# The ternary feed-forward phase of a two-layer transformer kernel: every second batch is rounded and clamped by POOL ahead of the turn

## The chip, the cores and the metric

The kernel runs on one core of one Trainium2 chip. The metric is device time in microseconds of one execution, as a median of several runs. Four engines compute: PE (TensorE, matrix products and transposes), ACT (ScalarE), DVE (VectorE) and POOL (GpSimd). They run their own instruction streams and meet at semaphores. SBUF is the on-chip memory that all of them reach; PE writes its results to PSUM.

## The reference, cut to what matters

Sixteen batches of 128 tokens with 128 features go through two layers, each a cross attention and a feed-forward part. The change touches only the last one, the feed-forward part of the second layer, whose activations are quantised to whole numbers:

```python
def _act_quant(x):
    scale = 127.0 / jnp.clip(jnp.max(jnp.abs(x), axis=-1, keepdims=True), 1e-05)
    xq = jnp.clip(jnp.round(x * scale), -128.0, 127.0) / scale
    return x + jax.lax.stop_gradient(xq - x)
...
gate = jax.nn.silu(_bitlinear(x, w_gate))        # 128 -> 512
up = _bitlinear(x, w_up)                         # 128 -> 512
return _bitlinear(gate * up, w_down)             # 512 -> 128, of the quantised product
```

So of every batch the product gate * up, 128 tokens by 512, gets one maximum per token, is multiplied by 127 over that maximum, rounded, clamped to -128..127, and multiplied with the last weight.

## The kernel before, in words

`main_kernel` calls five phases one after the other: `context`, `attention` of layer 0, `experts`, `attention` of layer 1, and `ternary_ffn`. The last is the one that the change edits. It begins at about 383 us of the span and holds all that follows.

`ternary_ffn` is a software pipeline over the 16 batches. Each engine has a function `step(h, r)`, and `run` (L1557) calls it for h = 0 to 20: steps 0 to 3 lie between the `head` parts, which turn and copy the input of four batches at a time, steps 4 to 7 are written out, steps 8 to 15 are two rounds of a hardware loop of four steps (`Fori`), and steps 16 to 20 are written out again. In step h each engine works on other batches, always in this order:

- PE: `gate_and_up` of batch h (L1711, L1712: two products 128x128 by 128x512 into `ps_gf` and `ps_uf`), `down` of batch h-5 (L1725: four products of the quantised, turned batch with the last weight, into `ps_df`), `turn` of batch h-3 (L1718: four transposes of `gr` into `ps_tf`).
- ACT: `copy_gu` of batch h-4 (L1679: `ps_tf` to `gq_t` in SBUF as bf16, with MAGIC subtracted), `round_gu` of batch h-3 (L1672: `gu` times `g_inv` plus MAGIC into `gr`; adding 1.5 times 2 to the 23rd leaves a float with no fraction, which is the rounding), `silu` of batch h (L1665: `ps_gf` to `gate`).
- DVE: `product` of batch h-1 (L1606: `ps_uf` times `gate` into `gu`), `clamp_gu` of batch h-4 (L1625: `gq_t` in place, bf16), `maximum` of batch h-1 (L1611), `tail` of batch h-5 (L1630: `ps_df` times `g_out`, added to `x_all`), and in each even step `scales` for two batches at once (L1618 `g_scl`, L1621 `g_inv`).
- POOL: once for two batches `g_out`, from `g_scl` (L1580), 128x2. Nothing else in the steps.
- SP stores a batch when its tail is done (L1743).

The buffers tie the engines: `gr`, `gq_t`, `gate` and each PSUM tile have two slots, `gu` has four. The clamp runs behind the turn, on the copied bf16 tile; since the transposed numbers are the rounded ones, it can stand on either side of it. An even batch is one with an even number; its scales come with those of the odd batch behind it.

Of the kernel before, what the change touches and what calls it, by code (L numbers as in the profile page):

```python
# [14 lines left out]
B = 16  # L15
# [1510 lines left out]
def ternary_ffn(nc, t, c):  # L1526
# [4 lines left out]
    with ExitStack() as ph:  # L1531
# [3 lines left out]
        def sem(name):  # L1535
# [15 lines left out]
            sem("clamp_ready"), sem("xt_done_f"), sem("xt_ready_f"))  # L1551
        gu_done, gate_ready, gu_ready, gmax_ready, gscl_step, gr_ready, gc_ready = (
            sem("gu_done"), sem("gate_ready"), sem("gu_ready"), sem("gmax_ready"), sem("gscl_step"), sem("gr_ready"), sem("gc_ready"))
        gt_done, gt_ready, d_done, out_ready = sem("gt_done"), sem("gt_ready"), sem("d_done"), sem("out_ready")
# [17 lines left out]
        @block.gpsimd  # L1572
        def _(pool):
            inputs.root(pool, NG - 1)
            w_down = c["w_scale"][:, 2:3].to_broadcast([P, 2])
            with pool.Fori(0, B // 4) as i:
                for pair in range(2):

                    pool.wait_ge(gscl_step, i * 4 + 2 * pair + 1)
                    pool.tensor_tensor(g_out[:, 2 * pair:2 * pair + 2], g_scl[:, 2 * pair:2 * pair + 2], w_down, ALU.mult)\  # L1580
                        .then_inc(out_scaled, 2)

        @block.vector
        def _(dve):
# [17 lines left out]
            def product(b, r):  # L1602
                wait(dve, gate_ready, b + 1)

                wait(dve, gr_ready, b - 3)
                dve.scalar_tensor_tensor(out=gu[:, r, :], in0=ps_u[:, r % 2, :], scalar=inputs.up_scl[:, bass.ds(b, 1)],  # L1606
                                         in1=gate[:, r % 2, :], op0=ALU.mult, op1=ALU.mult).then_inc(gu_ready, 1)

            def maximum(b, r):
                wait(dve, gu_ready, b + 1)  # L1610
                dve.tensor_reduce(g_max[:, r:r + 1], gu[:, r, :], AX_X, ALU.max, apply_absolute_value=True)\  # L1611
                   .then_inc(gmax_ready, 1)

# [12 lines left out]

# [21 lines left out]
        def _(act):  # L1648
# [43 lines left out]
        def _(pe):  # L1692
# [96 lines left out]
```

## Time and profile before

| What | us |
|---|---|
| median of 3 runs (lowest, highest) | 433.83 (432.37, 436.69) |
| the profiled execution: its time | 434.39 |
| its span, first to last instruction | 432.7 |
| of it the last phase, from about 383.2 on | 49.5 |
| product of the first and of the last batch start at | 388.29 and 421.02 |
| last instruction of DVE ends at | 430.45 |

The trace is of the profiled execution, and the times of its rows are microseconds from the start of the span. The execution's time is 1.7 us more than its span, and 0.56 us above the median. A view of busy time adds up instructions that can overlap at their ends: an instruction often starts before the one ahead of it on its engine has ended, so distances from start to start tell what an instruction takes out of its engine's time, and durations tell when a waiting engine may go.

### The profile page before, as it was taken

The numbers are of one execution on the slowest core, as the hardware profiler recorded it, in microseconds if no ns is written. First come the engines' busy times: TensorE is split into PE (matmuls) and PEld (weight loads), VectorE is DVE, ScalarE is ACT, GpSimd is POOL, SyncE is SP. The second block draws the span as 40 slices with busy tenths as digits, with TensorE's granted clock in tenths as the row PEclk, the third lists the DMA queues.
The fourth block names the chain that finished last, engine by engine and source line by source line (L and its number), as shares of the span: only waits on it lengthen the run. The fifth ranks groups of instructions, "written<-read, shape, count | busy, mean of one in ns | idle before, by whom it ended". The sixth has DMA issues, their size and how long they took to land. (4 is left out here: it accounts for less than half of the span.)

```text
span 432.7 us, 10420 instructions
## 1 busy us (share of the span) xinstructions
PE 359.2 (83%) x3434; PEld 258.3 (60%) x3434; DVE 288.3 (67%) x905; ACT 224.6 (52%) x420; POOL 90.2 (21%) x163
## 2 busy tenths in 40 slices
PE   2684779887877999999999999799899999756654
PEld 0452667776753677677767777566677676534433
DVE  6765768998946553663442443687789799367993
ACT  2152436665654745434343344055556656648993
POOL 7335131020211102101001001133333343310000
PEclk9886769999996999999999999889999999857996
DMA  7664954433144001630170100113443331000111
GB/s 215 138 157 111 226 165 129 130 117 111 55 124 148 2 2 40 126 80 2 36 208 12 36 0 0 37 31 104 122 127 113 101 100 28 3 1 1 32 30 37
DMA packets 54100, 34.98 MB, mean 81 GB/s; under 512 B 38744, under 2 KB 46256, under 8 KB 54064
## 3 DMA queue, kind: packets, MB, share of 16 engines
q1 hardware_dynamic: 44032, 31.43, 26.8%
q10 hardware_dynamic: 10032, 3.08, 3.0%
q8 instruction: 20, 0.33, 0.3%
q14 instruction: 16, 0.13, 0.1%
HBM read 24.60 MB, written 9.44 MB: 79 GB/s over the span
## 5 line engine op out<-in xcount | busy, mean ns | idle before, releaser
L1040 ACT ACTIVATE probs<-ps_e 128x512 f32<-128x512 f32 x128 | 74.6, 594 | 54.2 <-PE ps_e L885 49.7
L958 DVE TENSOR_REDUCE neg<-ps_s 128x4 f32<-128x512 f32 x128 | 85.1, 684 | 21.6 <-PE ps_s L868 20.1
L1286 DVE SCALAR_TENSOR_TENSOR x_all<-ps_ym,c_g,x_all 128x128 f32 (+1 forms) x128 | 36.0, 344 | 63.2 <-PE ps_ym L1381 63.0
L1381 PEld LDWEIGHTS ps_ym<-w,hid 128*128 128x128 f32 x512 | 60.8, 192 | 9.2 <-issue 6.7
L868 PE MATMUL ps_s<-k_rows,q_rows 96*128 96x128 bf16 x512 | 54.2, 234 | 10.6 <-DVE neg L958 4.9
L1381 PE MATMUL ps_ym<-w,hid 128*128 128x128 f32 x512 | 62.2, 276 | 0.0
L1371 PE MATMUL ps_h<-tok_t,w 128*128 (+1 forms) x128 | 62.1, 608 | 0.0
L1488 ACT ACTIVATE hid<-ps_h,b 128x512 f32<-128x512 f32 x64 | 43.1, 684 | 35.4 <-PE ps_h L1371 34.0
L868 PEld LDWEIGHTS ps_s<-k_rows,q_rows 96*128 96x128 bf16 x512 | 40.1, 104 | 24.1 <-issue 10.0
L885 PE MATMUL ps_e<-q_rows,k_rows 128*128 128x128 bf16 x512 | 51.2, 226 | 3.8 <-DMA q_rows<-neg_t 3.3
L885 PEld LDWEIGHTS ps_e<-q_rows,k_rows 128*128 128x128 bf16 x512 | 37.0, 101 | 9.1 <-DMA q_rows<-neg_t 3.9
L899 PE MATMUL ps_pv<-probs,v_aug 128*32 128x128 f32 x1024 | 36.5, 285 | 0.0
L1371 PEld LDWEIGHTS ps_h<-tok_t,w 128*128 128x128 f32 x128 | 22.6, 195 | 20.1 <-issue 14.9
L1093 POOL TENSOR_TENSOR v_aug<-v_all,zero 128x128 f32<-128x128 f32 x32 | 14.8, 463 | 88.4 <-PE ps_pv L899 87.2
L864 PE MATMUL ps_s<-upper,identb 128*128 128x512 bf16 x64 | 25.8, 403 | 4.6 <-PEq L1138 2.0
L899 PEld LDWEIGHTS ps_pv<-probs,v_aug 128*32 128x32 f32 x1024 | 27.0, 113 | 4.1 <-issue 0.4
L1052 ACT ACTIVATE neg_t<-ps_n 48x128 bf16<-48x128 bf16 x32 | 8.6, 269 | 35.3 <-PE ps_n L906 35.3
L1718 PE MATMUL ps_tf<-ident,gr 128*128 128x128 f32 x64 | 11.3, 303 | 14.2 <-ACT gr L1672 14.2
L925 PE MATMUL ps_y<-attn_w,oo_t 128*128 128x128 f32 x64 | 16.2, 336 | 7.5 <-ACT oo_t L1057 6.8
L984 DVE TENSOR_TENSOR x_all<-ps_y,x_all 128x128 f32<-128x128 f32 (+1 forms) x32 | 9.2, 287 | 16.7 <-PE ps_y L925 16.4
L1102 POOL TENSOR_SCALAR_AFFINE_SELECT probs<-probs 128x512 f32<-128x512 f32 x32 | 20.0, 625 | 0.0
L1045 ACT ACTIVATE o_t<-ps_pv 128x512 f32<-128x512 f32 x32 | 18.6, 580 | 2.1 <-PE ps_pv L899 2.0
(200 smaller groups left out, 555.7 us busy)
## 6 DMA issues: line engine op xcount, KB each, us to landing
k_rows<-k_dram SPq DMA_DIRECT2D x32, 144.0 KB
q_rows<-q_dram SPq DMA_DIRECT2D x32, 144.0 KB
k_rows<-k_dram SPq DMA_DIRECT2D x16, 288.0 KB
q_rows<-q_dram SPq DMA_DIRECT2D x16, 288.0 KB
k_dram<-parts SPq DMA_DIRECT2D x35, 128.0 KB, 2.5
w<-in_w SPq DMA_DIRECT2D x16, 128.0 KB, 2.7
q_dram<-parts SPq DMA_DIRECT2D x15, 128.0 KB, 2.2
q_dram<-parts ACTq DMA_DIRECT2D x9, 128.0 KB, 3.2
```

What stands on the lines that cost most here:

```text
L864: pe.matmul(ps_s[:, q % 2, :], identb[:], c["upper"][:].unsqueeze(1).to_broadcast([P, HQ, P]), start=True, stop=False, skip_group_check=True)
L868: last = pe.matmul(ps_s[:, q % 2, j * P:(j + 1) * P], q_rows[0:ROW_MAX, r, h, :], k_rows[0:ROW_MAX, r, h, :], start=(layer == 0), stop=Tru ...
L885: last = pe.matmul(ps_e[:, q % 2, j * P:(j + 1) * P], k_rows[:, r, h, :], q_rows[:, r, h, :], start=not masked, stop=True, skip_group_chec ...
L899: last = pe.matmul(ps_v[VW * j:VW * (j + 1), q * P:(q + 1) * P], v_aug[:, s, q * HQ + j, :], probs[:, s, q, j * P:(j + 1) * P], start=True ...
L958: dve.tensor_reduce(neg[:, s, q * HQ:(q + 1) * HQ], ps_s[:, q % 2, :].rearrange("p (h k) -> p h k", h=HQ), AX_X, ALU.max, negate=True).the ...
L1040: act.activation(probs[:, s, q, :], ps_e[:, q % 2, :], ACT.Exp, scale=SCALE).then_inc(exp_done, 1)
L1045: act.activation(o_t[:, s, :], ps_v[:], ACT.Copy).then_inc(ot_ready, 1)
L1102: pool.affine_select(out=probs[:, s, q, :], in_=probs[:, s, q, :], compare_op=ALU.is_ge, fill=0.0, base=0, pattern=[[0, HQ], [1, P]], chan ...
L1286: dve.scalar_tensor_tensor(out=batch_of(x_all, g * G + j), in0=ps_y[:, e % 2, j * D:(j + 1) * D], scalar=c_g[:, j, e:e + 1], in1=batch_of( ...
L1371: pe.matmul(ps_h[:, m, :], w1[:, e, m * P:(m + 1) * P], tok_t[:, bass.ds(g * GT, GT)], start=True, stop=True).then_inc(h_done, 1)
L1381: last = pe.matmul(ps_y[:, e % 2, j * D:(j + 1) * D], hid[:, (e % 2) * M + m, j * P:(j + 1) * P], w2[:, e, m, :], start=(m == 0), stop=(m ...
L1488: act.activation(hid[:, (e % 2) * M + m, :], ps_h[:, m, :], ACT.Gelu, bias=b1[:, e * M + m:e * M + m + 1]).then_inc(h_ready, 1)
```

## The change

For odd batches the rounding moves from ACT to POOL, and the clamp moves from DVE, behind the turn, to POOL, ahead of it: POOL reads `gu`, writes slot 1 of `gr`, waits for that, and clamps slot 1 in place, between MAGIC-128 and MAGIC+127, in 32-bit floats. Even batches stay as they were. POOL's hardware loop becomes eight written-out rounds.

The semaphores follow. `even_ready` and `odd_ready` take the place of `gr_ready`; `scale_step` takes that of `gmax_ready` and `gscl_step`, and `g_out` now waits for both scale instructions where it waited for the first. The rounding of an even batch waits for the scales of its pair, as before. An odd `down` waits for ACT's copy and for the tail two batches earlier.

```diff
@@ POOL @@
-            with pool.Fori(0, B // 4) as i:
-                for pair in range(2):
-
-                    pool.wait_ge(gscl_step, i * 4 + 2 * pair + 1)
-                    pool.tensor_tensor(g_out[:, 2 * pair:2 * pair + 2], g_scl[:, 2 * pair:2 * pair + 2], w_down, ALU.mult)\
-                        .then_inc(out_scaled, 2)
+            for pair in range(B // 2):
+                b, r = 2 * pair + 1, 2 * (pair % 2) + 1
+
+                pool.wait_ge(scale_step, 2 * b + 2)
+                pool.tensor_tensor(g_out[:, r - 1:r + 1], g_scl[:, r - 1:r + 1], w_down, ALU.mult).then_inc(out_scaled, 2)
+
+                wait(pool, gt_done, b - 1)
+                pool.tensor_scalar(gr[:, 1, :], gu[:, r, :], g_inv[:, r:r + 1], MAGIC, ALU.mult, ALU.add).then_inc(odd_ready, 1)
+                pool.wait_ge(odd_ready, b)
+                pool.tensor_scalar(gr[:, 1, :], gr[:, 1, :], MAGIC + 127.0, MAGIC - 128.0, ALU.min, ALU.max).then_inc(odd_ready, 1)
@@ DVE @@
-                wait(dve, gr_ready, b - 3)
+                if r % 2 == 0:
+                    wait(dve, even_ready, b - 2)
+                else:
+                    wait(dve, odd_ready, b - 3)
...
-                if exists(h - 4):
+                if exists(h - 4) and r % 2 == 0:
                     clamp_gu(h - 4, r % 2)
@@ ACT @@
-                if exists(h - 3):
+                if exists(h - 3) and (r - 3) % 2 == 0:
                     round_gu(h - 3, (r - 3) % 4)
@@ PE, turn @@
-                wait(pe, gr_ready, b + 1)
+                if s == 0:
+                    wait(pe, even_ready, b + 2)
+                else:
+                    wait(pe, odd_ready, b + 1)
@@ PE, down @@
-                wait(pe, gc_ready, b + 1)
+                if s == 0:
+                    wait(pe, gc_ready, b + 2)
+                else:
+                    wait(pe, gt_ready, b + 1)
+                    wait(pe, out_ready, b - 1)
```

What stands in a row on ACT in the middle of the hardware loop, two steps, before (`gq_t` is the copy, `gr` the rounding, `gate` the silu; the `L51` and `ISA` rows work out the value of a wait):

```order
L1679 ACTIVATE gq_t<-ps_tf,magic 128x512 [waits gt_done]
L1672 ACTIVATE gr<-gu,magic,g_inv 128x512 [waits gt_done,gscl_step]
L51 REGISTER_ALU
L1665 ISA [waits gu_ready,gu_done]
L1665 ACTIVATE gate<-ps_gf,in_gate_scl 128x512
L1679 ACTIVATE gq_t<-ps_tf,magic 128x512 [waits gt_done]
L1672 ACTIVATE gr<-gu,magic,g_inv 128x512 [waits gt_done,gscl_step]
L51 REGISTER_ALU
L1665 ISA [waits gu_ready,gu_done]
L1665 ACTIVATE gate<-ps_gf,in_gate_scl 128x512
```

And the same two steps now, an even step and an odd one:

```order
L1686 ACTIVATE gq_t<-ps_tf,magic 128x512 [waits gt_done]
L51 REGISTER_ALU
L1672 ISA [waits gu_ready,gu_done]
L1672 ACTIVATE gate<-ps_gf,in_gate_scl 128x512
L1686 ACTIVATE gq_t<-ps_tf,magic 128x512 [waits gt_done]
L51 ISA
L1679 ACTIVATE gr<-gu,magic,g_inv 128x512 [waits gt_done,scale_step_f]
L51 REGISTER_ALU
L1672 ISA [waits gu_ready,gu_done]
L1672 ACTIVATE gate<-ps_gf,in_gate_scl 128x512
```

The rounding is gone from the even step, in which batch h-3 is odd, and the copy and the silu follow each other there.

On DVE an even and an odd step in the middle of the loop stood like this before, from the product of one step to the tail of the next (`gu` is the product, `gq_t` the clamp, `g_max` the maximum, `x_all` the tail, `g_scl` and `g_inv` the scales):

```order
L1606 SCALAR_TENSOR_TENSOR gu<-ps_uf,in_up_scl,gate 128x512
L1625 TENSOR_SCALAR gq_t<-gq_t 128x512 [waits gt_ready]
L1611 TENSOR_REDUCE g_max<-gu 128x1 [waits gu_ready]
L1630 ISA [waits out_scaled,d_done]
L1630 SCALAR_TENSOR_TENSOR x_all<-ps_df,g_out,x_all 128x128
L1618 TENSOR_SCALAR g_scl<-g_max 128x2 [waits gmax_ready]
L1621 RECIPROCAL g_inv<-g_scl 128x2 [waits gscl_step]
L51 REGISTER_ALU
L1606 ISA [waits gr_ready,gate_ready]
L1606 SCALAR_TENSOR_TENSOR gu<-ps_uf,in_up_scl,gate 128x512
L1625 TENSOR_SCALAR gq_t<-gq_t 128x512 [waits gt_ready]
L1611 TENSOR_REDUCE g_max<-gu 128x1 [waits gu_ready]
```

And now:

```order
L1613 SCALAR_TENSOR_TENSOR gu<-ps_uf,in_up_scl,gate 128x512
L1632 TENSOR_SCALAR gq_t<-gq_t 128x512 [waits gt_ready]
L1618 TENSOR_REDUCE g_max<-gu 128x1 [waits gu_ready]
L1637 ISA [waits out_scaled,d_done]
L1637 SCALAR_TENSOR_TENSOR x_all<-ps_df,g_out,x_all 128x128
L51 REGISTER_ALU
L1625 TENSOR_SCALAR g_scl<-g_max 128x2 [waits scale_step_f]
L51 REGISTER_ALU
L1628 RECIPROCAL g_inv<-g_scl 128x2 [waits scale_step_f]
L1613 SCALAR_TENSOR_TENSOR gu<-ps_uf,in_up_scl,gate 128x512
L1618 TENSOR_REDUCE g_max<-gu 128x1 [waits gu_ready]
```

The clamp is gone from the odd step, the even step keeps it, and two register instructions have come in ahead of the scales.

On POOL, which had one instruction a pair, three now stand for every pair of batches:

```order
L1580 TENSOR_TENSOR g_out<-g_scl,w_scale 128x2 [waits scale_step_f]
L1583 TENSOR_SCALAR gr<-gu,g_inv 128x512 [waits gt_done]
L1585 TENSOR_SCALAR gr<-gr 128x512 [waits odd_ready]
L1580 TENSOR_TENSOR g_out<-g_scl,w_scale 128x2 [waits scale_step_f]
L1583 TENSOR_SCALAR gr<-gu,g_inv 128x512 [waits gt_done]
L1585 TENSOR_SCALAR gr<-gr 128x512 [waits odd_ready]
```

The two `TENSOR_SCALAR` rows are what left ACT and DVE; they lie between the `g_out` of one pair and that of the next.

## Rows read from the trace of the kernel before

**Rows 1.** Waits between 400 and 420 us: who waited, total us, times, longest.

```profile
PE ps_tf L1718 <- ACT gr L1672: 7.3, 9, 0.8
```

**Rows 2.** Timeline, ACT and PE in one step of the loop: start, duration, then idle before.

```profile
404.08 0.69 ACT L1679 ACTIVATE gq_t<-ps_tf,magic 128x512 bf16<-128x512 f32 x1 [0.17 <-PE ps_tf L1718]
404.67 0.80 ACT L1672 ACTIVATE gr<-gu,magic,g_inv 128x512 f32<-128x512 f32 x1
405.37 0.67 ACT L1665 ACTIVATE gate<-ps_gf,in_gate_scl 128x512 f32<-128x512 f32 x1
405.52 0.66 PE L1718 MATMUL ps_tf<-ident,gr 128*128 128x128 f32 x4 [0.82 <-ACT gr L1672]
406.22 0.69 ACT L1679 ACTIVATE gq_t<-ps_tf,magic 128x512 bf16<-128x512 f32 x1 [0.17 <-PE ps_tf L1718]
```

**Rows 3.** Timeline, DVE in two steps of the loop, even and odd; POOL beside it.

```profile
404.16 0.75 DVE L1606 SCALAR_TENSOR_TENSOR gu<-ps_uf,in_up_scl,gate 128x512 f32<-128x512 f32 x1 [0.35 <-ACT gate L1665]
404.83 0.28 DVE L1625 TENSOR_SCALAR gq_t<-gq_t 128x512 bf16<-128x512 bf16 x1
405.03 0.68 DVE L1611 TENSOR_REDUCE g_max<-gu 128x1 f32<-128x512 f32 x1
405.62 0.34 DVE L1630 SCALAR_TENSOR_TENSOR x_all<-ps_df,g_out,x_all 128x128 f32 x1
405.88 0.15 DVE L1618 TENSOR_SCALAR g_scl<-g_max 128x2 f32<-128x2 f32 x1
406.07 0.17 DVE L1621 RECIPROCAL g_inv<-g_scl 128x2 f32<-128x2 f32 x1
406.35 0.75 DVE L1606 SCALAR_TENSOR_TENSOR gu<-ps_uf,in_up_scl,gate 128x512 f32<-128x512 f32 x1
...
407.82 0.34 DVE L1630 SCALAR_TENSOR_TENSOR x_all<-ps_df,g_out,x_all 128x128 f32 x1
408.33 0.75 DVE L1606 SCALAR_TENSOR_TENSOR gu<-ps_uf,in_up_scl,gate 128x512 f32<-128x512 f32 x1 [0.17 <-ACT gate L1665]
...
406.18 0.19 POOL L1580 TENSOR_TENSOR g_out<-g_scl,w_scale 128x2 f32<-128x2 f32 x1 [4.01 <-DVE g_scl L1618]
```

**Rows 4.** Timeline, DVE in the written-out steps ahead of the loop.

```profile
395.41 0.75 DVE L1606 SCALAR_TENSOR_TENSOR gu<-ps_uf,in_up_scl,gate 128x512 f32<-128x512 f32 x1 [1.06 <-ACT gate L1665]
...
401.79 0.17 DVE L1621 RECIPROCAL g_inv<-g_scl 128x2 f32<-128x2 f32 x1
401.87 0.75 DVE L1606 SCALAR_TENSOR_TENSOR gu<-ps_uf,in_up_scl,gate 128x512 f32<-128x512 f32 x1
```

**Rows 5.** Groups of POOL's instructions, whole span: count | busy us, mean ns.

```profile
L1102 POOL TENSOR_SCALAR_AFFINE_SELECT probs<-probs 128x512 f32<-128x512 f32 x32 | 20.0, 625 | 0.0
L225 POOL TENSOR_TENSOR q_rest<-q_full,parts 128x512 f32<-128x512 f32 x4 | 4.6, 1160 | 46.6 <-ACT q_full L220 46.6
L195 POOL TENSOR_TENSOR q_rstd<-q_vareps,half 128x4 f32<-128x4 f32 x4 | 4.0, 1009 | 46.8 <-DVE q_vareps L101 46.8
L1580 POOL TENSOR_TENSOR g_out<-g_scl,w_scale 128x2 f32<-128x2 f32 x8 | 1.6, 194 | 36.6 <-DVE g_inv L1621 19.4 <-DVE g_scl L1618 17.1
```

**Rows 6.** Timeline near 54 us, POOL and DVE side by side.

```profile
52.41 4.51 POOL L1115 TENSOR_TENSOR x_all<-x_all,row_bias 128x2048 f32<-128x2048 f32 x1
...
53.80 0.69 DVE L958 TENSOR_REDUCE neg<-ps_s 128x4 f32<-128x512 f32 x1 [0.21 <-PE ps_s L868]
...
54.53 2.42 DVE L965 CAST neg_parts<-neg 128x16 bf16<-128x16 f32 x1
```

**Rows 7.** Timeline of DVE and PE behind the last product.

```profile
421.02 0.75 DVE L1606 SCALAR_TENSOR_TENSOR gu<-ps_uf,in_up_scl,gate 128x512 f32<-128x512 f32 x1
...
423.13 0.17 DVE L1621 RECIPROCAL g_inv<-g_scl 128x2 f32<-128x2 f32 x1
...
427.23 1.11 PE L1718 MATMUL ps_tf<-ident,gr 128*128 128x128 f32 x4 [1.05 <-ACT gr L1672]
...
430.10 0.35 DVE L1630 SCALAR_TENSOR_TENSOR x_all<-ps_df,g_out,x_all 128x128 f32<-128x128 f32 x1 [0.44 <-PE ps_df L1725]
```

More of the change, by code:

```diff
@@ L1551, in ternary_ffn @@
             sem("clamp_ready"), sem("xt_done_f"), sem("xt_ready_f"))
-        gu_done, gate_ready, gu_ready, gmax_ready, gscl_step, gr_ready, gc_ready = (
-            sem("gu_done"), sem("gate_ready"), sem("gu_ready"), sem("gmax_ready"), sem("gscl_step"), sem("gr_ready"), sem("gc_ready"))
+        gu_done, gate_ready, gu_ready, scale_step, even_ready, odd_ready, gc_ready = (
+            sem("gu_done"), sem("gate_ready"), sem("gu_ready"), sem("scale_step_f"), sem("even_ready"), sem("odd_ready"), sem("gc_ready"))
         gt_done, gt_ready, d_done, out_ready = sem("gt_done"), sem("gt_ready"), sem("d_done"), sem("out_ready")
@@ L1611, in maximum @@
                 dve.tensor_reduce(g_max[:, r:r + 1], gu[:, r, :], AX_X, ALU.max, apply_absolute_value=True)\
-                   .then_inc(gmax_ready, 1)
+                   .then_inc(scale_step, 1)
             def scales(b, r):
                 pair = slice(r - 1, r + 1)
-                wait(dve, gmax_ready, b + 1)
+                wait(dve, scale_step, b * 2)
                 dve.tensor_scalar(g_scl[:, pair], g_max[:, pair], 1e-5, 1.0 / 127.0, ALU.max, ALU.mult)\
-                   .then_inc(gscl_step, 1)
-                wait(dve, gscl_step, b - 1 + 1)
-                dve.reciprocal(g_inv[:, pair], g_scl[:, pair]).then_inc(gscl_step, 1)
+                   .then_inc(scale_step, 1)
+                wait(dve, scale_step, b * 2 + 1)
+                dve.reciprocal(g_inv[:, pair], g_scl[:, pair]).then_inc(scale_step, 1)
             def clamp_gu(b, s):
                 wait(dve, gt_ready, b + 1)
-                dve.tensor_scalar(gq_t[:, s, :], gq_t[:, s, :], 127.0, -128.0, ALU.min, ALU.max).then_inc(gc_ready, 1)
+                dve.tensor_scalar(gq_t[:, s, :], gq_t[:, s, :], 127.0, -128.0, ALU.min, ALU.max).then_inc(gc_ready, 2)
             def tail(b, r):
@@ L1668, in round_gu @@
             def round_gu(b, r):
-                wait(act, gscl_step, b + 2 - r % 2)
+                wait(act, scale_step, b * 2 + 4)
                 wait(act, gt_done, b - 1)
                 act.activation(gr[:, r % 2, :], gu[:, r, :], ACT.Identity, bias=magic[:, 0:1], scale=g_inv[:, r:r + 1])\
-                   .then_inc(gr_ready, 1)
+                   .then_inc(even_ready, 2)
             def copy_gu(b, s):
```

## The prediction, made blind

> **What bounds the phase now.** I read the waits between engines first, then the timeline of one step, engine by engine, since the change lies wholly in the last 49.5 us. In the waits PE stands 7.3 us of 20 for ACT's rounding [rows 1]. The timeline shows the ring behind it: copy at 404.08, rounding at 404.67, turn at 405.52, next copy at 406.22 [rows 2]. One step is 406.22 - 404.08 = 2.14 us: 0.59 from copy to rounding, 0.80 + 0.05 until the turn starts, 0.66 for the turn, 0.04 until the copy may start. ACT stands idle 0.17 of it. So ring and ACT are nearly equal: ACT alone needs 0.59 + 0.70 + (0.85 - 0.17 = 0.68) = 1.97.
>
> DVE is almost as full. Its even step, with the scales, is 406.35 - 404.16 = 2.19 us and waits for nothing; its odd step is 408.33 - 406.35 = 1.98, with a wait for ACT's silu in it [rows 3]. So the reader is to see two full engines and a ring, 4.27 us for two steps, and a DVE that sets the limit as soon as ring and ACT are relieved.
>
> **ACT and PE after the change.** A rounding (0.70 from start to start) leaves every second step. ACT then needs 2 x 0.59 + 2 x 0.68 + 0.70 = 3.24 us for two steps. The ring through ACT and PE is broken at odd batches. PE issues the same work; its odd `down` waits for the tail two batches earlier, which DVE does two steps before, so I cost this wait at nothing; behind it in PE's queue is the turn of an odd batch, and if the wait did bind, the copy would be late by as much.
>
> **DVE after the change.** Even step: unchanged at 2.19. Two register instructions come ahead of the scales and one may come ahead of the product. They are hidden where the engine is still busy with the tail; otherwise each can cost about 0.06 (the loop costs 0.20 for its register work: reciprocal to product is 406.35 - 406.07 = 0.28 in the loop [rows 3], but 401.87 - 401.79 = 0.08 outside of it [rows 4]). I take 0.06 for the pair, between 0 and 0.12. Odd step: the clamp goes, but what it frees is small. Product to maximum is 405.03 - 404.16 = 0.87 with the clamp between; without it the maximum still waits for the product's end, 0.75 + 0.04 = 0.79. So a clamp of 0.28 busy gives back 0.08. The step is 0.79 + 0.59 (maximum to tail) + tail to next product. That last term is hidden behind a wait in the trace: at least 0.26 (tail to `g_scl`), at most 0.51 (407.82 to 408.33) [rows 3]. I take 0.26 + 0.20 of register work = 0.46, so 1.84. Two steps: 2.19 + 1.84 + 0.06 = 4.09.
>
> - Loop, product 7 to product 15: 421.02 - 404.16 = 16.86 now [rows 3, 7], 4 x 4.09 = 16.36 then: -0.5 (bounds -1.5 with 0.26 and no register cost, 0 if DVE stays as long as the ring).
> - Written-out steps, product 3 to product 7: 404.16 - 395.41 = 8.75 now [rows 3, 4]. Without register work a pair is (2.19 - 0.20) + (0.79 + 0.59 + 0.26) = 3.63, two are 7.26. The first clamp still waits for the same copy and product 7 may wait for its silu, so I count -1.3 of the -1.5.
>
> **The tail.** Now: last product 421.02, end of the last tail 430.10 + 0.35 = 430.45, so 9.43 [rows 7]. In it ACT rounds batches 13, 14 and 15 one behind the other, each in the ring. Then: the reciprocal ends 423.13 + 0.17 - 421.02 = 2.28 behind the product. ACT rounds batch 14 at once (2.32 to 3.12), PE turns it from 3.17, at up to the 1.11 of the last turn (0.66 in the loop: PE's matrix clock has fallen there), so until about 4.2 [rows 2, 7]. Meanwhile POOL starts `g_out` 0.15 behind its releaser (406.18 against 405.88 + 0.15) and needs 0.19 [rows 3], and then twice d, the unknown duration of its new instructions, with 0.05 behind each: batch 15 is ready at 2.28 + 0.15 + 0.19 + 0.10 + 2d = 2.72 + 2d. With d = 0.75 that is 4.2, equal to PE. From turn to end the rows give 430.45 - 427.23 = 3.22 [rows 7], less a clamp and its wait, 0.28 + 0.04 [rows 3]: 2.90. Total 7.1 to 7.2: -2.25.
>
> **POOL's instructions.** The trace has none of this kind. Nearest from below is a one-input instruction of the same 128x512 floats, in place, at 0.625 us; from above a two-input one at 1.160 us [rows 5]. Rounding has one tensor input and a scalar per token, clamping one tensor input and two constants, so I go near the lower row: d = 0.85. That it may lie outside is shown by the power on 128x4, 1.009 us for four columns [rows 5]: this engine's price hangs on the operation. Against d = 0.75 my value costs 2 x 0.1 in the tail: +0.2.
>
> POOL's work must also fit. Counted from the reciprocal's start: 0.17 + 0.15 + 0.15 (`g_out`, its overlap off) + d + 0.05 + d = 0.52 + 2d. The next even step's clamp on DVE comes 0.28 + 1.84 + 0.67 = 2.79 after it, and the turn, which waits for POOL, about there too. So up to d = 1.13 nothing is late but the tail. This clamp is what counts, for the trace shows that POOL can hold DVE up: a CAST of 128x16 took 2.42 us, from 54.53 to 56.95, while a POOL instruction ran from 52.41 to 56.92; a reduction beside the same instruction took its usual 0.69 [rows 6]. Products, maxima and tails read at most one tensor from SBUF, like that reduction from PSUM; clamp and `g_scl` are of the CAST's kind.
>
> The Trainium skill says so as a rule ("SBUF — State Buffer", Who interferes with whom): a DVE instruction in a two-port mode and a GpSimd instruction exclude each other for their whole length, and reductions never contend. Rows 6 agree (2.42 us against 0.69). It leaves the sum at d = 0.85, where POOL is done 0.57 before the clamp, but it sets where rival 2 begins: with it at d = 1.13; without it only POOL's own ring of two instructions, a turn of 0.66 and three waits of 0.05 would have to stay under 4.09, so up to d = 1.64.
>
> **Sum.** -1.3 - 0.5 - 2.25 + 0.2 = -3.85 us. The profiled execution is 434.39, so 430.5; it lies 0.56 above the median, and from the median 433.83 the same step leads to 430.0. I give 430.2.
>
> **Rivals** (from 433.8).
> 1. DVE gains nothing in the loop: tail to product is 0.51 or more and the registers show, so a pair stays near 4.27. For it: DVE waits only 0.17 in an odd step [rows 3]. Against it: even then the written-out steps and the tail gain. Time: with half of the written-out steps' gain, 0.65, and 2.05 in the tail it is 431.1; with 1.3 in all, 432.5. Chance 0.2.
> 2. POOL is the new bound, the case on the other side. From d = 1.13 on each pair is longer by 2d - 2.27, since DVE's clamp has to wait for POOL, and with it all of DVE's queue. Over some 6.5 pairs and with 2(d - 0.75) in the tail: d = 1.16 gives +0.3 + 0.8 on top of -4.05, so 430.9; d = 1.37 gives +3.1 + 1.2, no gain left, 434; d = 1.6 gives +6.0 + 1.7, so 437.5. Above 1.37 the kernel is slower than before. For it: the 1.160 and 1.009 rows; against it: 0.625. Chance that d exceeds 1.37: 0.15, that it exceeds 1.65 (over 1% slower): 0.1. A rule of the Trainium skill leads here ("GPSIMD Engine Reference", Key points): for elementwise work DVE is about twice as fast. DVE reads a 128x512 float tile in 0.68 in its reduction [rows 3]; twice that would be an estimate of 1.36 for d, just the point where nothing is gained. The same page's section Engine selection calls one-input work roughly line-rate, and the 0.625 row agrees with that.
> 3. More than forecast: no register cost, tail to product 0.3, PE still at its full clock in the tail. -1.5 - 1.3 - 2.6 = -5.4: 428.4. Chance 0.1.
>
> The forecast (429 to 431.2) has 0.55. One per cent, about what a measurement here can tell from no change, is 4.3 us, and my sum ends short of it: of the forecast's chance I count 0.2 beyond the line, and rival 3's 0.1. So faster 0.3, within 1% 0.6, slower 0.1. The range 428.8 to 434.8 leaves out some 0.08 below and 0.12 above.
>
> **What would show it.** Right: roundings on ACT eight, PE's wait for them about halved, DVE waiting for almost nothing in the loop with a pair near 4.1; POOL's two instructions at 0.65 to 1.1 each; the last turn within 5 us of the last product, the last clamp gone from the chain. Wrong: `TENSOR_SCALAR` on POOL above 1.2, DVE clamps of over 0.5 that end with a POOL instruction, or the turn of odd batches waiting for POOL; and for rival 1 a DVE pair at 4.25 with no waits.

## The result, and the profile after

The changed kernel ran in 428.60 us in the median of four runs (426.15 to 431.78), the kernel before in 434.38 (432.37 to 436.69) beside it. The ratio is 0.9854, with an interval of 0.981 to 0.9897: faster, by 4.5 to 8.2 us, where I had 3.85. A second, longer comparison, told of below, gave 0.988 (0.9838 to 0.9922). Ratios, here and below, leave out runs that lay over 1.5% above the fastest of their kernel. The profiled execution took 427.59 us with a span of 425.9, against 434.39 and 432.7.

So 6.8 us of span are gone. I cut both traces at the same instructions to see where:

| Stretch, us | before | after | change | predicted |
|---|---|---|---|---|
| start of the last phase (first instruction of DVE in it) | 383.26 | 380.77 | -2.49 | 0 |
| from there to the first product | 5.03 | 5.04 | 0 | 0 |
| product 0 to product 3 | 7.12 | 6.68 | -0.44 | 0 |
| product 3 to product 7, written-out steps | 8.75 | 8.77 | 0 | -1.3 |
| product 7 to product 15, hardware loop | 16.86 | 15.62 | -1.24 | -0.5 |
| last product to the end of the last tail | 9.43 | 6.55 | -2.88 | -2.05 |

Two things catch the eye. A third of the gain lies ahead of the phase, in code that the change leaves alone. And inside the phase no term that I had priced has the size that I gave it: their sum, -4.5, is near my -3.85 only because the misses have both signs.

The waits that bound the kernel before, in the view that answers to [rows 1], here for 400 to 416 us:

```profile
PE ps_tf L1728 <- ACT gr L1679: 5.7, 4, 1.4
ACT gr L1679 <- DVE g_inv L1628: 0.9, 2, 0.5
```

PE waits for ACT's rounding four times in these 16 us, where it was seven times before, but each wait is longer, and the total is 5.7 us both times: the sum of PE's waits does not show the gain, and the sign "PE's wait for them about halved" came in their number alone. What is new is the second row: ACT now waits for DVE's reciprocal, which it never did before in this phase.

DVE in two steps of the loop, to be laid beside [rows 3]:

```profile
404.93 0.34 DVE L1637 SCALAR_TENSOR_TENSOR x_all<-ps_df,g_out,x_all 128x128 f32 x1
405.19 0.74 DVE L1613 SCALAR_TENSOR_TENSOR gu<-ps_uf,in_up_scl,gate 128x512 f32<-128x512 f32 x1
405.91 0.29 DVE L1632 TENSOR_SCALAR gq_t<-gq_t 128x512 bf16<-128x512 bf16 x1
406.12 0.68 DVE L1618 TENSOR_REDUCE g_max<-gu 128x1 f32<-128x512 f32 x1
406.72 0.34 DVE L1637 SCALAR_TENSOR_TENSOR x_all<-ps_df,g_out,x_all 128x128 f32 x1
406.97 0.16 DVE L1625 TENSOR_SCALAR g_scl<-g_max 128x2 f32<-128x2 f32 x1
407.17 0.17 DVE L1628 RECIPROCAL g_inv<-g_scl 128x2 f32<-128x2 f32 x1
407.45 0.75 DVE L1613 SCALAR_TENSOR_TENSOR gu<-ps_uf,in_up_scl,gate 128x512 f32<-128x512 f32 x1
408.23 0.69 DVE L1618 TENSOR_REDUCE g_max<-gu 128x1 f32<-128x512 f32 x1
408.84 0.34 DVE L1637 SCALAR_TENSOR_TENSOR x_all<-ps_df,g_out,x_all 128x128 f32 x1
409.10 0.74 DVE L1613 SCALAR_TENSOR_TENSOR gu<-ps_uf,in_up_scl,gate 128x512 f32<-128x512 f32 x1
409.77 0.29 DVE L1632 TENSOR_SCALAR gq_t<-gq_t 128x512 bf16<-128x512 bf16 x1
```

No row names a wait. The even step, 405.19 to 407.45, is 2.26 (2.19 before), the odd one, 407.45 to 409.10, is 1.65 (1.98 before). Two steps are 3.91, where I had 4.09. Read the odd step by its parts: product to maximum 0.78 (I had 0.79), maximum to tail 0.61 (0.59), tail to next product 0.26, where I had taken 0.46. That one number is nearly the loop's whole miss; with the 0.01 of the maximum and 2.26 for my 2.25 it gives 0.18 a pair.

ACT and PE beside it; shown are the rounding of an even batch, its turn and its copy:

```profile
407.42 0.81 ACT L1679 ACTIVATE gr<-gu,magic,g_inv 128x512 f32<-128x512 f32 x1 [0.46 <-DVE g_inv L1628]
408.29 0.66 PE L1728 MATMUL ps_tf<-ident,gr 128*128 128x128 f32 x4 [1.38 <-ACT gr L1679]
408.98 0.69 ACT L1686 ACTIVATE gq_t<-ps_tf,magic 128x512 bf16<-128x512 f32 x1 [0.17 <-PE ps_tf L1728]
```

The rounding starts 0.08 behind the end of DVE's reciprocal (407.17 + 0.17), and the copy ends at 409.67, 0.10 ahead of the clamp at 409.77 that needs it. So the ring of waits did not vanish: it now runs from DVE's reciprocal through ACT and PE to DVE's next clamp. The experiments come back to it.

POOL's groups, from 380 us on, for [rows 5]:

```profile
L1583 POOL TENSOR_SCALAR gr<-gu,g_inv 128x512 f32<-128x512 f32 x8 | 5.5, 691 | 0.0
L1585 POOL TENSOR_SCALAR gr<-gr 128x512 f32<-128x512 f32 x8 | 4.9, 613 | 0.7
```

The unknown of the prediction is known: 0.691 us for the rounding, 0.613 for the clamp. The clamp takes about what the affine select on a tile of that size took, 0.625. The kernel before also has this same instruction, two constants on 128x512 floats, on DVE, where it takes 0.415; POOL needs 1.5 times that:

```profile
L1590 DVE TENSOR_SCALAR tok_tk<-tok_tk 128x512 f32<-128x512 f32 x4 | 1.7, 415 | 0.0
```

The end, for [rows 7]:

```profile
416.88 0.74 DVE L1613 SCALAR_TENSOR_TENSOR gu<-ps_uf,in_up_scl,gate 128x512 f32<-128x512 f32 x1
...
418.81 0.17 DVE L1628 RECIPROCAL g_inv<-g_scl 128x2 f32<-128x2 f32 x1
...
419.93 0.66 PE L1728 MATMUL ps_tf<-ident,gr 128*128 128x128 f32 x4 [1.62 <-ACT gr L1679]
...
420.74 0.91 PE L1728 MATMUL ps_tf<-ident,gr 128*128 128x128 f32 x4
...
423.08 0.35 DVE L1637 SCALAR_TENSOR_TENSOR x_all<-ps_df,g_out,x_all 128x128 f32<-128x128 f32 x1 [0.32 <-PE ps_df L1739]
```

The two last turns follow each other at once, at 0.66 and 0.91 us, where the last one before took 1.11 and stood alone. The second of them starts at 420.74, 0.06 behind POOL's last clamp (420.07 to 420.68): it is POOL's chain, and not the turn of batch 14, that ends last in the tail.

### The profile page after: what moved, and what is told of

It reads as the page before. It is cut to its first block and busy times, and to the rows that moved or that the text cites. A ratio compares the mean times of both kernels' runs of the same rounds, so it can differ in the third digit from the quotient of the medians.

```text
span 425.9 us, 10418 instructions
## 1 busy us (share of the span) xinstructions
PE 354.5 (83%) x3432; PEld 255.7 (60%) x3434; DVE 286.5 (67%) x897; ACT 219.1 (51%) x412; POOL 100.6 (24%) x179
## 5 line engine op out<-in xcount | busy, mean ns | idle before, releaser
L1093 POOL TENSOR_TENSOR v_aug<-v_all,zero 128x128 f32<-128x128 f32 x32 | 14.7, 462 | 88.1 <-PE ps_pv L899 87.0
L912 PE MATMUL ps_o<-ident,o_t 128*128 128x128 f32 x128 | 19.7, 277 | 0.0
```

The costliest lines, as they stand in the source:

```text
L912: last = pe.transpose(ps_o[:, q * P:(q + 1) * P], o_t[:, s, q * P:(q + 1) * P], ident[:])
```

## The experiments

Each trace is measured between the same instructions as the first two. "Clock" is PE's mean granted clock between product 3 and 7, and behind the last product; 1.00 is the 2.4 GHz level, 0.50 the level of 1.2 GHz.

| Kernel | ratio to before (interval) | phase starts | 3 to 7 (clock) | 7 to 15 | tail (clock) | whole phase |
|---|---|---|---|---|---|---|
| before | | 383.26 | 8.75 (1.00) | 16.86 | 9.43 (0.70) | 47.19 |
| before, again | 0.9976 (0.9937, 1.0014) | 380.45 | 9.59 (0.82) | 16.87 | 9.06 (0.82) | 47.21 |
| changed | 0.9854 (0.981, 0.9897) | 380.77 | 8.77 (0.74) | 15.62 | 6.55 (0.82) | 42.66 |
| changed, again | 0.988 (0.9838, 0.9922) | 380.79 | 7.80 (1.00) | 15.61 | 6.09 (1.00) | 41.65 |
| round only | 0.9895 (0.9857, 0.9934) | 382.25 | 8.07 (1.00) | 15.97 | 6.24 (1.00) | 42.42 |
| clamp only | 1.0187 (1.0139, 1.0236) | 382.43 | 11.55 (0.58) | 21.07 | 10.60 (0.66) | 55.36 |
| one clamp more | 0.9865 (0.9821, 0.991) | 381.52 | 7.81 (0.82) | 15.92 | 7.00 (0.87) | 42.41 |
| two clamps more | 0.9938 (0.9901, 0.9976) | 383.44 | 8.79 (0.74) | 16.62 | 8.15 (0.69) | 45.28 |
| no clamp | 0.983 (0.9791, 0.9868) | 379.74 | 8.03 (0.74) | 15.08 | 5.83 (1.00) | 40.86 |
| 15 alone on POOL | 0.9962 (0.9932, 0.9992) | 381.13 | 9.51 (0.82) | 16.89 | 7.88 (0.64) | 46.43 |
| 13 and 15 on POOL | 0.9919 (0.9888, 0.9951) | 383.17 | 9.24 (0.82) | 16.86 | 7.25 (0.77) | 45.50 |
| written out, before | 0.9995 (0.996, 1.003) | 381.42 | 10.37 (0.50) | 17.53 | 9.53 (0.69) | 49.36 |
| written out, changed | 0.9886 (0.9843, 0.9928) | 383.99 | 7.64 (1.00) | 15.43 | 6.29 (1.00) | 41.51 |
| written out, no clamp | 0.981 (0.9758, 0.9862) | 384.05 | 7.00 (1.00) | 14.24 | 6.14 (0.83) | 39.53 |

### Does the change act ahead of its phase? Both kernels again

No edit in either.

> The kernel before, unchanged, once more. In the first pair of traces 6.8 us of span went, of which only 4.5 lie in the last phase (383.26 to 430.45 before, 380.77 to 423.43 after); the other 2.3 lie ahead of it, where both kernels are the same. Theory A (that part is chance, set by where PE's clock falls near the end of the second attention): ratio 1.00 within 0.5%, and the start of the last phase moves by 1 us or more against 383.26 in this trace, while the distance of product 7 to product 15 stays 16.8 to 16.9 us and the tail 9.2 to 9.6. Theory B (the change also moves code or transfers ahead of the phase): the phase again starts at 383.0 to 383.5.

> The changed kernel, unchanged, with more rounds. Theory A: ratio 0.988 to 0.991, that is 4 to 5 us, what the phase alone gives, and the phase starts somewhere between 380.5 and 384. Theory B: ratio 0.984 to 0.986 and the phase starts at 380.5 to 381.2 again. By both product 7 to product 15 is 15.6 us (bound by DVE) and product 3 to product 7 is 8.8 if PE's granted clock is 0.5 in these steps as in the first trace of this kernel, but near 7.5 if it is 1.0.

Theory A holds by the kernel before: it now reaches the phase at 380.45, 2.8 us earlier than in its first trace, and with the same 47.2 us in the phase itself (its tail is 9.06, 0.1 under what I expected). Its medians in this comparison are 434.20 and 434.24. The changed kernel alone would not have decided: it started at 380.79, within 0.02 of its first trace, as theory B had it too. Over all fourteen traces of the table the start lies between 379.7 and 384.1 in no order that goes with the edits. The windows of 4 us near the end of the second attention show what part of it is. First trace of the kernel before (columns: length, then busy us and count of PE, PE's loads, DVE, ACT and POOL, then PE's clock and the transfers' share and rate):

```profile
368.00:372.00 4.00, 3.12 (x39) 2.55 (x42) 1.56 (x6) 2.69 (x7) 2.48 (x6) 0.78 0.01 3
372.00:376.00 4.00, 3.48 (x41) 2.40 (x33) 0.78 (x4) 1.85 (x4) 1.46 (x4) 0.79 0.00 0
```

And its second trace:

```profile
368.00:372.00 4.00, 3.48 (x57) 2.75 (x57) 1.63 (x6) 2.85 (x8) 2.63 (x5) 1.00 0.01 3
372.00:376.00 4.00, 2.74 (x44) 1.95 (x44) 2.40 (x8) 3.01 (x7) 0.76 (x2) 1.00 0.02 4
```

The same code ran at a granted clock of 0.78 and 0.79 of full speed once, and of 1.00 the next time. What that costs is read between two additions that DVE makes in both traces, first trace, then second:

```profile
369.70 0.29 DVE L984 TENSOR_TENSOR x_all<-ps_y,x_all 128x128 f32<-128x128 f32 x1 [1.97 <-PE ps_y L925]
375.26 0.29 DVE L984 TENSOR_TENSOR x_all<-ps_y,x_all 128x128 f32<-128x128 f32 x1 [3.18 <-PE ps_y L925]
...
368.60 0.29 DVE L984 TENSOR_TENSOR x_all<-ps_y,x_all 128x128 f32<-128x128 f32 x1 [1.97 <-PE ps_y L925]
372.60 0.29 DVE L984 TENSOR_TENSOR x_all<-ps_y,x_all 128x128 f32<-128x128 f32 x1 [1.63 <-PE ps_y L925]
```

The stretch takes 5.56 us at a mean clock of 0.69, and 4.00 at 1.00. That is 1.6 of the 2.8 us; 1.1 were there at its start already. The changed kernel shows both too: 4.00 at 1.00 in its first trace, 5.55 at 0.69 in its second, which still starts the phase as early because it was 1.7 us ahead at the stretch's start.

So 2.5 of the 6.8 us between the first two traces say nothing on the change. Its own effect is the difference of the phase: 47.19 and 47.21 against 42.66 and 41.65, on the mean 5.0 us, or 1.2%. Both measured ratios have that in their intervals.

The second trace of the changed kernel settles the written-out steps too. Against the first trace of the kernel before, with the clock at 1.00 in both, product 3 to 7 is 8.75 before and 7.80 changed. The -1.3 that I gave this term was -0.95, and the zero of the first pair went with a low clock in the changed kernel:

```profile
394.00:398.00 4.00, 3.80 (x22) 2.63 (x21) 3.43 (x8) 3.26 (x6) 1.48 (x3) 0.61 0.02 5
```

in its first trace, against its second:

```profile
394.00:398.00 4.00, 2.46 (x21) 1.72 (x21) 3.76 (x10) 3.50 (x7) 1.48 (x3) 1.00 0.02 5
```

### Which half pays? Rounding alone, clamp alone

`round only`: POOL rounds the odd batches, and DVE clamps all of them as before (not shown: `down` again waits for the clamp of every batch).

```diff
-                pool.tensor_scalar(gr[:, 1, :], gu[:, r, :], g_inv[:, r:r + 1], MAGIC, ALU.mult, ALU.add).then_inc(odd_ready, 1)
-                pool.wait_ge(odd_ready, b)
-                pool.tensor_scalar(gr[:, 1, :], gr[:, 1, :], MAGIC + 127.0, MAGIC - 128.0, ALU.min, ALU.max).then_inc(odd_ready, 1)
+                pool.tensor_scalar(gr[:, 1, :], gu[:, r, :], g_inv[:, r:r + 1], MAGIC, ALU.mult, ALU.add).then_inc(odd_ready, 2)
...
-                if exists(h - 4) and r % 2 == 0:
+                if exists(h - 4):
                     clamp_gu(h - 4, r % 2)
```

> Changed kernel, but POOL only rounds the odd batches; DVE clamps all batches behind the turn as before. Theory A (DVE sets the pace once ring and ACT are relieved, and a clamp costs it only 0.09 to 0.2 a step): product 7 to product 15 is 15.9 to 16.7 us, between the two; tail 6.4 to 7.0, since POOL's clamp (0.66) and DVE's (0.34) there nearly exchange; ratio 0.989 to 0.992. Theory C (the clamp is what made the loop faster): product 7 to 15 is 16.8 or more.

Product 7 to 15 is 15.97, the tail 6.24, a little under what I expected. Theory A holds: relieving ACT brings 0.9 of the loop's 1.25, the clamp 0.35, which is 0.09 for each of four odd clamps, as product and maximum have it. In the whole phase, at full clock from product 3 on in both, the clamp is worth 42.42 - 41.65 = 0.8 us; the ratios, 0.9895 and 0.988, can't tell the two kernels apart. So most of the gain is the rounding's. The trace also shows the exclusion of [rows 6] at work. DVE's clamp of an odd batch and POOL's rounding beside it, DVE first:

```profile
397.12 0.58 DVE L1630 TENSOR_SCALAR gq_t<-gq_t 128x512 bf16<-128x512 bf16 x1
...
405.33 0.36 DVE L1630 TENSOR_SCALAR gq_t<-gq_t 128x512 bf16<-128x512 bf16 x1
```

and POOL:

```profile
396.86 0.69 POOL L1583 TENSOR_SCALAR gr<-gu,g_inv 128x512 f32<-128x512 f32 x1
...
404.84 0.70 POOL L1583 TENSOR_SCALAR gr<-gu,g_inv 128x512 f32<-128x512 f32 x1
```

The clamp takes 0.58 in place of 0.28 and ends at 397.70, 0.15 behind the end of POOL's rounding (397.55); the other one takes 0.36 and ends at 405.69, again 0.15 behind POOL's 405.54. All six clamps of this trace that start under a rounding of POOL do so: they take 0.36 to 0.58 and end 0.14 or 0.15 behind it. The changed kernel avoids it, since DVE has no clamp in the steps in which POOL works.

`clamp only`: ACT rounds all batches, and POOL clamps the odd ones in `gr`, ahead of the turn (not shown: which scales and which semaphore an odd rounding goes by).

```diff
-                wait(pool, gt_done, b - 1)
-                pool.tensor_scalar(gr[:, 1, :], gu[:, r, :], g_inv[:, r:r + 1], MAGIC, ALU.mult, ALU.add).then_inc(odd_ready, 1)
                 pool.wait_ge(odd_ready, b)
...
-                if exists(h - 3) and (r - 3) % 2 == 0:
+                if exists(h - 3):
                     round_gu(h - 3, (r - 3) % 4)
```

> Changed kernel, but ACT rounds all batches, as before; POOL only clamps the odd ones in gr ahead of the turn. If the ring of ACT and PE was the bound (rounding, turn, copy), POOL's clamp now stands inside it in every second step: about 0.61 + 0.15 longer for a pair, so product 7 to product 15 goes from 16.86 to 19 to 20 us and the ratio is 1.006 to 1.012. If DVE was the bound already (so that the clamp taken off it is what pays), product 7 to 15 falls to 16.4 or less and the ratio is below 0.998.

The sign is as the ring has it, the size is more than I expected: 21.07 for the loop, a ratio of 1.0187. The chain of waits shows POOL inside the ring, and a turn at the low clock level (1.13 for 0.66) behind 1.5 us in which PE had nothing to do; the granted clock between products 7 and 15 was 0.90 on the mean, against 1.00 in the loop of both main kernels:

```profile
412.13 0.81 ACT gr L1677
412.94 0.08 issue
413.02 0.62 POOL gr L1583
413.64 0.04 issue
413.69 1.13 PE ps_tf L1726 x4
```

So the clamp taken off DVE is worth nothing as long as ACT rounds all batches, and a POOL instruction in the path from rounding to turn costs more than its 0.61 us: the loop is 4.2 us longer than the kernel before's, 1.05 for each pair. How much of that is the low clock no run separates. The change works because POOL does the whole of an odd batch, beside ACT and not behind it.

### How much more could POOL take? The clamp issued again

```diff
                 pool.tensor_scalar(gr[:, 1, :], gr[:, 1, :], MAGIC + 127.0, MAGIC - 128.0, ALU.min, ALU.max).then_inc(odd_ready, 1)
+                pool.wait_ge(odd_ready, 4 * pair + 3)
+                pool.tensor_scalar(gr[:, 1, :], gr[:, 1, :], MAGIC + 127.0, MAGIC - 128.0, ALU.min, ALU.max).then_inc(odd_ready, 1)
```

with the counts that others wait for raised to four for each odd batch; the second form has this once more.

> Changed kernel with POOL's clamp issued twice (the second changes nothing), 0.66 us more on POOL for each pair. POOL is then done some 2.55 us behind the start of the reciprocal, just ahead of DVE's clamp of the next even step at 2.67. By my account of POOL's slack the loop keeps its time (product 7 to 15: 15.6 to 15.8) and only the tail grows by about 0.6: ratio 0.2% above that of the changed kernel. If POOL had no slack: product 7 to 15 grows by 0.5 or more for each pair, 17.5 or more.

> POOL's clamp issued three times, 1.35 us more a pair; POOL is busy until 3.25 us behind the reciprocal. Theory L (a POOL instruction keeps DVE's clamp waiting until it ends): DVE's clamps show durations or starts that end with POOL's third clamp, late by 0.5 to 0.7 in each pair; product 7 to product 15 is 17.5 to 18.8 us. Theory R (no such exclusion, only the ring POOL, turn, which is about 3.6 us for a pair and under 3.9): product 7 to 15 stays 15.6 to 16.0 and only the tail grows, by about 1.3.

One clamp more gives 15.92 in the loop, 0.1 above what I expected, and a tail of 7.00. The 0.3 lies in the loop's first pair, 4.37 us at a clock of 0.93; the other three, at 1.00, are 3.83, 3.89 and 3.83, no longer than the changed kernel's. The slack is there. Two more cost the loop 1.0 us, between the two theories' ranges, and neither theory has the reason. Theory L wanted DVE's clamps late behind POOL; their longest is 0.33. What happens is this. DVE first:

```profile
408.38 0.75 DVE L1617 SCALAR_TENSOR_TENSOR gu<-ps_uf,in_up_scl,gate 128x512 f32<-128x512 f32 x1 [0.44 <-ACT gate L1676]
412.96 0.29 DVE L1636 TENSOR_SCALAR gq_t<-gq_t 128x512 bf16<-128x512 bf16 x1
```

PE and ACT:

```profile
405.48 0.66 PE L1732 MATMUL ps_tf<-ident,gr 128*128 128x128 f32 x4 [0.99 <-POOL gr L1589]
406.18 0.69 ACT L1690 ACTIVATE gq_t<-ps_tf,magic 128x512 bf16<-128x512 f32 x1 [1.01 <-PE ps_tf L1732]
407.47 0.68 ACT L1676 ACTIVATE gate<-ps_gf,in_gate_scl 128x512 f32<-128x512 f32 x1
```

and POOL, the third clamp of the next pair:

```profile
413.01 0.71 POOL L1589 TENSOR_SCALAR gr<-gr 128x512 f32<-128x512 f32 x1
```

The odd turn at 405.48 waits for POOL, ACT's copy of it waits until 406.18, and the rounding and the silu, which have nothing to do with that batch, stand behind the copy in ACT's queue; so the product waits 0.44 for its silu. It is a wait passed on by an engine that works in order. The exclusion shows only the other way round: DVE's clamp began at 412.96, and POOL's, from 413.01, took 0.71 in place of 0.61. Rival 2's price was a pair longer by 2d - 2.27. With 0.69 + 3 x 0.61 = 2.52 for 2d that is 0.25 a pair, 1.0 for the loop's four, and 1.0 is what the loop lost; but it came by another path than the one I had named, every second pair being 4.4 us and the others 3.9, so the agreement is luck.

### The tail: batch 15 alone, then 13 and 15

The kernel before, with POOL doing batch 15, and in a second form also 13; the rest as before (`LAST` stands for these batches; in the second form POOL's hardware loop is written out as well):

```diff
+                        pool.wait_ge(gscl_step, b + 1)
+                        pool.wait_ge(gt_done, b - 1)
+                        pool.tensor_scalar(gr[:, 1, :], gu[:, b % 4, :], g_inv[:, b % 4:b % 4 + 1], MAGIC, ALU.mult, ALU.add)\
+                            .then_inc(xt_done, 1)
+                        pool.wait_ge(xt_done, done + 1)
+                        pool.tensor_scalar(gr[:, 1, :], gr[:, 1, :], MAGIC + 127.0, MAGIC - 128.0, ALU.min, ALU.max)\
+                            .then_inc(xt_done, 1)
...
-                if exists(h - 3):
+                if exists(h - 3) and not h - 3 in LAST:
                     round_gu(h - 3, (r - 3) % 4)
```

> Kernel before, with batch 15 alone rounded and clamped by POOL ahead of its turn; all others as before. If the tail's gain comes from batch 15 no longer standing behind batch 14 on ACT, and the loop's gain is another matter: last product to last tail falls from 9.43 to 6.5 to 7.0, product 7 to product 15 stays 16.8 to 16.9, the time falls by 2.5 to 3 us (ratio 0.993 to 0.995). If the tail is short in the changed kernel only since PE's clock holds longer there: the tail stays above 8 and the ratio is 0.997 or more.

> Kernel before, with batches 13 and 15 on POOL (15 alone brought the tail only from 9.06 to 9.43 down to 7.88, since batch 14's rounding still stood behind the turn and copy of 13 on ACT, and PE's granted clock had fallen by its turn). If that is the reason, with 13 off ACT too the rounding of 14 starts within 0.1 us of the reciprocal's end, its turn still runs at the high clock (0.66 us), and the tail is 6.1 to 6.8, as in the changed kernel; product 7 to 15 stays 16.7 to 16.9; the time falls by 2.4 to 3.0 us, ratio 0.993 to 0.995. If the short tail needs the rest of the change, it stays above 7.2.

Batch 15 alone gives 7.88, a gain of 1.2 to 1.6 us (from 9.06 or 9.43) where I expected 2.4 to 2.9, at a ratio of 0.9962. Batch 14's rounding still stood behind the turn and the copy of 13. With 13 on POOL too it starts at the reciprocal's end, but the tail is 7.25 and not 6.1 to 6.8, just above the 7.2 that I had set as the mark for "the short tail needs the rest of the change":

```profile
423.73 0.81 ACT L1682 ACTIVATE gr<-gu,magic,g_inv 128x512 f32<-128x512 f32 x1 [0.82 <-DVE g_inv L1631]
424.60 1.05 PE L1733 MATMUL ps_tf<-ident,gr 128*128 128x128 f32 x4 [1.58 <-ACT gr L1682]
```

The rounding is 0.03 behind the reciprocal (423.53 + 0.17), as it should be. The turn takes 1.05 instead of 0.66: in this run the clock had fallen by then, in the second trace of the changed kernel it stayed at 1.00 to the end. Against that trace, with its 6.09, the 1.16 us are mostly this: both last turns take 1.05 or 1.06 for 0.66 and the products behind them some 0.6 for 0.4. Another 0.2 is a reciprocal that ends 2.28 behind the last product in place of 2.11, behind a clamp of DVE that starts 0.85 behind the product in place of 0.68. So of the tail's 2.9 us some 1.8 to 2.2 are the order of work in the last batches (9.06 to 9.43 down to 7.25), and most of the rest goes with PE's clock. Whether the change holds the clock up is not shown. The eight traces in which POOL rounds every odd batch have 0.82 to 1.00 behind the last product, but for the 0.69 with two clamps more; the six in which ACT rounds in the loop have 0.64 to 0.82.

### Does DVE set the pace? Steps written out, clamps left out

```diff
-            with eng.Fori(2, B // 4) as i:
-                for j in range(4):
-                    step(i * 4 + j, j)
+            for h in range(8, B):
+                step(h, h % 4)
```

`no clamp` leaves out the clamp to -128..127, on POOL and on DVE. The largest value of a row is 127 by the division, so nothing is clipped. On POOL the rounding then counts for two, and every `down` waits as an odd one does (not shown).

```diff
-                pool.wait_ge(odd_ready, b)
-                pool.tensor_scalar(gr[:, 1, :], gr[:, 1, :], MAGIC + 127.0, MAGIC - 128.0, ALU.min, ALU.max).then_inc(odd_ready, 1)
...
-                if exists(h - 4) and r % 2 == 0:
-                    clamp_gu(h - 4, r % 2)
```

> Changed kernel without any clamp of the rounded products, on POOL or DVE (left out: the clamp to -128..127; the values are at most 127 already, since each row is divided by its own maximum, so the output does not change by it). If DVE sets the pace in the loop, an even step gets 0.09 shorter (product to maximum 0.78 in place of 0.86): product 7 to product 15 falls by 0.3 to 0.6 from 15.6, and the tail by 0.3 to 1.0 (POOL's 0.66 goes, PE's turn of batch 14 then comes last): ratio 0.2 to 0.3% below that of the changed kernel. If something else paces the loop, product 7 to 15 stays 15.6.

> Changed kernel with steps 8 to 15 written out, so that no register work stands ahead of the waits. Reciprocal to next product is 0.28 to 0.30 in the loop and 0.08 outside. If DVE paces the loop, each pair gets 0.2 shorter: product 7 to product 15 falls from 15.6 to 14.7 to 15.0 us, the time by 0.6 to 0.9 us. If ring or ACT pace it, it stays at 15.4 or more.

> Kernel before with steps 8 to 15 written out. If the ring ACT, PE paces it (2.135 us a step), product 7 to product 15 stays 16.7 to 17.0 and the ratio is 1.00 within 0.3%. If DVE's register work did, it falls by 0.6 or more.

> Changed kernel, written out and without the clamps (left out: the clamp to -128..127, which changes no value here). Product 7 to 15: 15.08 without clamps, less 0.8 by writing out: 14.2 to 14.5 us, if DVE still paces; tail 5.6 to 6.2. Time 425.5 to 426.5, ratio 0.978 to 0.982 to the kernel before. If ACT (3.24 us a pair and its waits) becomes the bound, product 7 to 15 stays at 14.8 or more.

The kernel before does not care: ratio 0.9995. Its loop read 17.53, missing its 16.7 to 17.0, because its first pair took 4.73 at a clock of 0.93; the last three pairs are 4.27, 4.27 and 4.26, the ring to the digit. The changed kernel cared less than expected: 15.43 in place of 14.7 to 15.0, and above the 15.4 that I had named as the sign of a ring. The written-out form shows why:

```profile
405.91 0.17 DVE L1627 RECIPROCAL g_inv<-g_scl 128x2 f32<-128x2 f32 x1
406.00 0.75 DVE L1612 SCALAR_TENSOR_TENSOR gu<-ps_uf,in_up_scl,gate 128x512 f32<-128x512 f32 x1
...
407.64 0.74 DVE L1612 SCALAR_TENSOR_TENSOR gu<-ps_uf,in_up_scl,gate 128x512 f32<-128x512 f32 x1
408.51 0.29 DVE L1631 TENSOR_SCALAR gq_t<-gq_t 128x512 bf16<-128x512 bf16 x1
...
409.77 0.17 DVE L1627 RECIPROCAL g_inv<-g_scl 128x2 f32<-128x2 f32 x1
```

and ACT's copy ahead of that clamp:

```profile
407.72 0.69 ACT L1685 ACTIVATE gq_t<-ps_tf,magic 128x512 bf16<-128x512 f32 x1 [0.17 <-PE ps_tf L1727]
```

Reciprocal to product is 0.09 now, as expected, but product to clamp has grown from 0.67 to 0.87: the clamp starts 0.10 behind the copy's end (408.41), the same distance as in the loop. From one reciprocal to the next is 3.86: reciprocal, rounding of the even batch, turn, copy, and DVE's clamp 2.60 later, then maximum, tail, `g_scl` and the next reciprocal, 1.26. This is the ring through DVE. In the loop it is 3.85 to 3.93 from one reciprocal to the next as well, so DVE's own work with its register instructions and the ring end together, and taking one away frees only 0.2 us of the loop. With the clamps gone the ring has lost its last link: written out and without clamps a pair is 3.56, which is DVE's own work, and the loop is 14.24, within what was expected.

Leaving the clamps out in the loop form gives 15.08 and a ratio of 0.983 (0.9791 to 0.9868) to the kernel before, with 426.87 us; written out 0.981 (0.9758 to 0.9862). Both phases, 40.86 and 39.53 us, are shorter than the changed kernel's 42.66 and 41.65. By the whole time no clamp beats the kernel before clearly; against the changed kernel the intervals overlap, and it is the phase that says it is ahead.

## Why the prediction was wrong

The median of 428.6 lies 0.2 us under the range's lower end, 428.8, and the first comparison is clear of one per cent, to which I gave only 0.3 (the second, up to 0.9922, is not). The mechanism held; two terms of the sum were too small, the loop by 0.7 and the tail by 0.8, and the written-out steps 0.35 too large. Point by point:

- **What bounds the kernel** was right. The ring of rounding, turn and copy paced the loop at 4.27 us a pair (written out: 4.27 still), and DVE was just behind it. `round only` has 0.9 of the loop's 1.25 us, and `clamp only` is slower by 1.9%: the rounding was the part to move.
- **The loop, "tail to next product ... I take 0.26 + 0.20 of register work = 0.46"**: this step failed. Its cost is 0.26, the lower of the two bounds that I had. The register instructions behind a tail cost nothing: the next product starts 0.26 behind a tail that takes 0.34, in the loop and written out. Behind the short reciprocal they do show (0.28 in the loop against 0.09 written out). Four pairs at 0.18 less are 0.7, and with the 0.5 that I had counted they make the loop's 1.24. My bound of -1.5 had it inside. What the prediction did not have is the ring through DVE's clamp: 3.86 us a pair written out, just under the 3.91 of the loop. It did not change the loop's time, but it is why writing the steps out brought 0.2 and not 0.6 to 0.9.
- **The tail, "-2.25" and "+0.2"**: this step failed in size, by 0.8, the mechanism as told: with d = 0.85 POOL's chain ends last, and it did. Three parts were too dear. d was 0.69 and 0.61 instead of 0.85 twice, 0.4. The reciprocal ends 2.10 behind the last product (418.81 + 0.17 - 416.88), not 2.28, 0.2. From the last turn's start to the end it is 423.43 - 420.74 = 2.69, not 2.90, with a turn of 0.91 where the trace before had 1.11, 0.2. The turn of batch 14, 0.66 where I allowed 1.11, is not in this sum, since POOL ended later.
- **The written-out steps, "-1.3"**: -0.95 at equal clocks, from one trace of each kernel; what took the rest is open.
- **POOL's slack** was right: nothing but the last turn was late behind it, and one clamp more could be added at no cost in the pairs that ran at full clock.
- **The exclusion of DVE and POOL** was right in kind, by the round-only kernel's 0.58, and of no effect in the changed kernel, as said.
- **No gain in the loop (rival 1)** did not come: a pair is 3.91. **POOL as the bound (rival 2)** did not come either, since 2d is 1.30 and not 2.27. Its estimate of 1.36 for d doubled the 0.68 of DVE's reduction; DVE's row for the same instruction, 0.415, was in the trace, and twice that is 0.83. **More than forecast (rival 3)**, at 0.1, is what happened in its direction, with 5.0 us in the phase for its 5.4: of its conditions, tail to product of 0.3 was met, PE at its full clock in the tail was met in the second trace and not in the first, and no register cost was not met (the even step is 2.26).
- **The range** allowed for no chance in the measurement. The phase starts at 379.7 to 384.1 in fourteen traces whose code is the same up to there, so single traces differ by up to 4.3 us without any edit. The effect read in the phase, 5.0 us, taken from 433.83, is 428.8, just on the range's lower end: that the median fell outside and not inside is chance, that it was so near the end is not.

## What to carry to other kernels

When two engines and a ring all stand near the same period, price each of them after the change from its own distances, and look for the ring that closes next, through which instruction of the engine just relieved. A term hidden behind a wait has two bounds; look first at whether its instructions can run while the engine is still busy, for then the lower one holds. And cut two traces at the same instructions before the difference of their spans is believed: here a third of it lay in code that nobody had touched.

## What the runs showed of the hardware

- POOL's `TENSOR_SCALAR` on 128x512 floats: 0.69 us with a multiplier for each partition, 0.61 with two constants, about the same as its affine select of that size (0.625) and a little over half of its two-input instruction (1.160). DVE's `TENSOR_SCALAR` with two constants on that size took 0.415.
- POOL and a DVE clamp of bf16 in SBUF exclude each other in either direction: DVE's took 0.36 to 0.58 for 0.28, ending 0.14 or 0.15 behind POOL; POOL's 0.71 for 0.61 when DVE's had begun 0.05 earlier. Products, maxima and tails beside POOL kept their durations. The Trainium skill ("SBUF — State Buffer", Who interferes with whom) says that whoever issues first keeps the shared ports for its whole instruction and the other is blocked. These rows agree in kind, in both orders; in size they show less, since POOL lost 0.10 us where the clamp had 0.24 still to run.
- The granted clock of PE in the same stretch of the same program differs between executions: 0.69 or 1.00 in one stretch of the second attention, with 5.56 and 4.00 us for the same work. Between products 3 and 7 a lower clock went with 0.8 us more in the kernel before (0.82 against 1.00) and with 1.0 in the changed one (0.74 against 1.00).
